# Decoder kernel on one core: the causal mask moves to VectorE, normalisations are pipelined, and the cross attention's softmax goes by row tiles

## The chip, the cores and the metric

The kernel runs on one core of a Trainium2 chip. The metric is device time in microseconds for one execution of the whole program, taken as the median of several runs. TensorE (PE) does the matmuls, VectorE (DVE) and ScalarE (ACT) the elementwise work, GpSimd (POOL) copies, powers and indirect DMAs, and SyncE (SP) issues most DMAs.

## What is computed

Two decoder layers over x of 8 sequences x 256 tokens x 256 features. Each layer is an attention, a second (cross) attention and a routed feed-forward part, each fed by a layer normalisation and added to x:

```
x = x + L0_attn(layernorm(x))            # causal self attention, 16 heads, 4 key heads, head size 128
x = x + L0_xattn(layernorm(x), ctx)      # top-2 of 64 context rows
x = x + L0_ffn(layernorm(x))             # 16 experts, 4 chosen
x = x + L1_attn(layernorm(x))            # gated delta rule, 64-step state
x = x + L1_xattn(layernorm(x), ctx)      # cross attention, keys = 64 context rows + 256 tokens
x = x + L1_ffn(layernorm(x))             # 128 experts, 48 kept, 8 chosen

def _layernorm(x, eps=1e-05):
    return (x - mean(x)) / sqrt(var(x) + eps)

# L0_attn
scores = einsum('bkgqd,bksd->bkgqs', qg, k) * scale
causal = triu(full((S, S), -inf), k=1)
attn = softmax(scores + causal)
out = einsum('bkgqs,bksd->bkgqd', attn, v)

# L1_xattn
q = rope(rms_norm(q, q_norm_w)); k = rope(rms_norm(k, k_norm_w))
probs = softmax(einsum('bhqd,bhkd->bhqk', q, k) * SCALE)
attn = einsum('bhqk,bhkd->bhqd', probs, v)
```

## The kernel before

Everything is in 32-bit floats. x lies in SBUF as 16 row tiles of 128 tokens. The program is a row of blocks, with all engines meeting between two blocks; within a block each engine has its own queue, in the order in which the code is written, and semaphores tie the queues together. There is no scheduler: the order of the code is the order of the queues.

`layernorm` (L155) is called six times, in 4 turns of 4 row tiles. A turn is one chain: VectorE's statistics (L181, L184) and the add of epsilon (L186), GpSimd's power for the reciprocal root (L200), VectorE's four normalisations (L191), eight transposes on TensorE into two PSUM banks (L213), and ScalarE's copy to `xnT` (L223). VectorE begins a turn's normalisations only when the transposes of the turn before have been made, and the transposes of a turn begin when its copy of the turn before is stored.

`attention` (L271) serves both the self attention (`cross` false) and the cross attention (`cross` true). A unit is one group of 4 query heads with one key head, for one sequence; there are 32 units, two at a time in buffers h = 0 and 1. The function `schedule` gives every engine the same row of stages. `stage(h, front, back)` does the front half of one unit (projections, rotation, and in the cross attention the root mean square of queries and keys, then transposes of queries and keys) and the back half of the unit before it, in the other buffer (scores, softmax, transposes of the probabilities, the product with the values, the output product). So a stage takes one unit forward, and there are some 32 of them in each attention.

In the back half the heads go by pairs, 0 and 1, then 2 and 3. On TensorE: scores of two heads, a projection of the front unit, the transposes of the probabilities (`turn_probs`, L460), the product with the values (`mix`, L470), then the same for heads 2 and 3, and `give` (L478). On VectorE: `row_max` for two heads (L588 in the cross attention, L594 in the self attention), which makes `mx` and the negated bound `nb`; ScalarE's `exps` (L684) writes `probs` and its row sums `den`; VectorE's `norm_probs` (L602 reciprocal, L605 multiply); `keep_probs` on VectorE (L614, L616) and ScalarE (L691, L694) copies the transposed probabilities out of PSUM. VectorE's `rotate` (L540 to L542) stands between the pairs for the queries, and for keys and values (part `TB`) between the normalisations of head 2 and head 3. ScalarE's `keep_v` (L666 to L671) waits for this last rotation and stands between its copies of the probabilities of heads 2 and 3.

A head's scores are two row tiles of 128 queries. In the cross attention each has 320 keys. In the self attention tile 0 sees 128 keys and tile 1 sees 256; both tiles lie in one PSUM bank, and the causal mask gets there first, by a bf16 matmul of an identity with a table of zeros and -1e30 (L448), onto which the score matmuls accumulate. In the cross attention GpSimd raises 15 columns of sums of squares to the power -1/2 (L388); VectorE's `rms_keys` (L576, L580) waits for it, and the transposes of queries and keys (L434, L437) wait for `rms_keys`.

## Time and profile before

| what | us |
|---|---|
| median of 3 runs (4133.5 to 4137.38) | 4135.25 |
| the profiled execution, its own time | 4131.25 |
| its span | 4129.5 |
| TensorE busy / VectorE busy / ScalarE busy / GpSimd busy | 3545.6 / 2634.8 / 1641.9 / 1414.0 |
| self attention, 26.47 to 664.00: TensorE / VectorE / ScalarE busy | 576.0 / 387.4 / 254.6 |
| 100 us of the cross attention, 3200 to 3300: TensorE / VectorE / ScalarE busy | 90.2 / 61.7 / 41.2 |
| first layer normalisation, 0 to 26.47: TensorE / VectorE busy | 7.8 / 13.1 |

The span is cut into stages: first normalisation to 26, self attention to 666, set attention to 759, routed experts from 780 to 1120, delta attention to 2882, cross attention from 2935 to 3861, sparse experts to the end. The second to sixth normalisations lie between these. A wait is read from a row's square bracket: how long the engine was idle ahead of it, and which engine's instruction ended that. TensorE's clock was granted in full (1.00) throughout both attentions' steady parts.

### The profile page before, as it was taken

The page shows a single profiled execution, that of the slowest core. Times are in us where ns is not written, and L with a number is a line of the kernel's source. Part 1 is how long each engine was busy: PE and PEld are TensorE (multiplying, and loading weights), DVE is VectorE, ACT ScalarE, POOL GpSimd, SP SyncE. Part 2 cuts the span into 40 slices and gives each one's busy share as a digit, 9 for nine tenths or more (in the row PEclk, how much of TensorE's full clock was granted, in tenths as well). Part 3 has the DMA queues.
Part 4 walks back from the last instruction along what each step waited for, and adds up shares of the span by engine and source line. Part 5 has one row for each costly group of instructions (what it writes and reads, how often), then busy time and mean ns, then how long its engine had stood idle before and what let it go on. Part 6 is the DMA issues. An engine that isn't in the chain of part 4 may idle for free. (4 is left out here: it accounts for less than half of the span.)

```text
span 4129.5 us, 57677 instructions
## 1 busy us (share of the span) xinstructions
PE 3545.6 (86%) x17488; PEld 2734.0 (66%) x17488; DVE 2634.8 (64%) x7558; ACT 1641.9 (40%) x4218; POOL 1414.0 (34%) x2085
## 2 busy tenths in 40 slices
PE   7999996589677999999999999997499999999564
PEld 5667665455365888888888888886355556556453
DVE  5666665532247888888888888873666666666531
ACT  3444432133234445555455554541244444444221
POOL 0000000068515555555555555552111111111055
PEclk9999998599869999999999999999699999999666
DMA  2000003345500111111111111110100000000346
GB/s 76 0 0 0 0 0 88 96 71 85 115 12 20 41 25 40 30 35 36 29 37 27 38 28 38 26 21 20 48 1 0 0 0 0 0 0 0 117 111 143
DMA packets 220951, 150.05 MB, mean 36 GB/s; under 512 B 116976, under 2 KB 208656, under 8 KB 220208
## 3 DMA queue, kind: packets, MB, share of 16 engines
q1 hardware_dynamic: 193664, 111.55, 10.4%
q0 software_dynamic: 22848, 31.69, 4.7%
q10 hardware_dynamic: 4224, 4.19, 0.3%
q8 instruction: 104, 1.70, 0.2%
q14 instruction: 111, 0.91, 0.1%
HBM read 105.71 MB, written 41.61 MB: 36 GB/s over the span
## 5 line engine op out<-in xcount | busy, mean ns | idle before, releaser
L1926 DVE SCALAR_TENSOR_TENSOR dl_y<-ps,dl_taps,dl_y 128x255 f32<-128x255 f32 (+2 forms) x1536 | 653.1, 475 | 129.5 <-ACT dl_y L1822 125.3
L1657 PE MATMUL ps<-xnT,dl_wkqv 128*128 128x256 f32 x2048 | 540.7, 390 | 32.4 <-DVE dl_lp L1969 22.3
L1657 PEld LDWEIGHTS ps<-xnT,dl_wkqv 128*128 128x128 f32 x2048 | 366.9, 193 | 83.9 <-issue 37.2
L388 POOL TENSOR_TENSOR at_rs<-at_ss,mhalf 128x15 f32<-128x15 f32 x32 | 125.5, 3922 | 744.8 <-DVE at_ss L571 744.8
L1580 POOL TENSOR_TENSOR dl_rn<-dl_n,mhalf 128x4 f32<-128x4 f32 x128 | 173.5, 1355 | 550.6 <-DVE dl_n L1942 550.6
L470 PE MATMUL ps<-at_shared,at_v 128*128 128x256 f32 (+2 forms) x1280 | 314.2, 378 | 4.6
L1822 ACT ACTIVATE dl_y<-ps,dl_taps 128x256 f32<-128x256 f32 x512 | 260.1, 560 | 101.0 <-PE ps L1657 101.0
L414 PE MATMUL ps<-at_wq,at_xb 128*128 (+1 forms) x512 | 244.4, 611 | 36.0 <-POOL at_xb L382 33.9
L1598 POOL TENSOR_TENSOR dl_inv_u<-dl_inv_u,dl_inv_tmp 64x30 f32<-64x30 f32 (+14 forms) x480 | 260.0, 542 | 37.6
L470 PEld LDWEIGHTS ps<-at_shared,at_v 128*128 128x128 f32 (+1 forms) x1280 | 209.7, 189 | 88.8 <-issue 64.0
L450 PE MATMUL ps<-at_kT,at_qT 128*128 128x320 f32 (+2 forms) x1024 | 257.7, 385 | 1.4 <-ACT at_kT L676 1.4
L460 PE MATMUL ps<-ident,at_probs 128*128 128x128 f32 (+1 forms) x1152 | 172.3, 281 | 100.2 <-DVE at_probs L605 100.2
L478 PE MATMUL ps<-at_wo,at_oT 128*128 (+1 forms) x1024 | 234.8, 382 | 18.7 <-ACT at_oT L699 18.7
L1682 PE MATMUL ps<-dl_wo,dl_z 128*128 128x256 f32 x1024 | 243.2, 380 | 0.0
L1595 POOL TENSOR_TENSOR dl_inv_tmp<-dl_inv_u,dl_inv_a 64x30 f32<-64x30 f32 (+14 forms) x480 | 234.2, 488 | 24.7
L460 PEld LDWEIGHTS ps<-ident,at_probs 128*128 128x128 f32 (+1 forms) x1152 | 122.9, 134 | 173.5 <-DVE at_probs L605 160.6
L1830 ACT ACTIVATE dl_z<-dl_y 128x512 f32<-128x512 f32 x256 | 161.6, 631 | 190.5 <-DVE dl_y L1926 190.5
L380 POOL COPY at_xb<-xnT 128x512 f32 (+1 forms) x64 | 39.2, 612 | 560.8 <-PE ps L422 556.0
L478 PEld LDWEIGHTS ps<-at_wo,at_oT 128*128 128x128 f32 x1024 | 189.4, 190 | 54.7 <-issue 27.5
L1668 PE MATMUL ps<-dl_z 128*128 128x512 f32 (+1 forms) x512 | 224.0, 520 | 0.0
L588 DVE TENSOR_REDUCE at_mx<-ps 128x2 f32<-128x640 f32 x128 | 105.6, 825 | 180.3 <-PE ps L450 176.7
L450 PEld LDWEIGHTS ps<-at_kT,at_qT 128*128 128x128 f32 x1024 | 169.3, 191 | 68.6 <-ACT at_kT L676 11.9
(348 smaller groups left out, 7755.5 us busy)
## 6 DMA issues: line engine op xcount, KB each, us to landing
dl_grow<-decay_rows SPq DMA_DIRECT2D x128, 128.0 KB, 3.0
sp_wgu<-in_w1gu SPq DMA_DIRECT2D x12, 768.0 KB
dl_wkqv<-in_w1kqv SPq DMA_DIRECT2D x16, 512.0 KB, 4.6
delta_diag<-dl_lp SPq DMA_DIRECT2D x512, 8.0 KB
dl_diag<-delta_diag_tt SPq DMA_DIRECT2D x512, 8.0 KB, 1.7
moe_wgu<-in_w0gu SPq DMA_DIRECT2D x16, 448.0 KB, 11.5
sp_wd<-in_w1d SPq DMA_DIRECT2D x12, 384.0 KB
dl_wo<-in_w1o SPq DMA_DIRECT2D x16, 256.0 KB, 3.7
```

The costliest lines, as they stand in the source:

```text
L414: last = nc.tensor.matmul(k.ps[h][:, t, :], xb[h][:, c, t * P:(t + 1) * P], wq[:, c, ds(group(u) * (G * HD), G * HD)], start=c == 0, stop= ...
L450: last = nc.tensor.matmul(scores(h, r, t), qT[h][:, r, t * P:(t + 1) * P], kT[h][:, 0:seen(t)], start=cross, stop=cross or t == TB - 1)
L460: last = nc.tensor.transpose(slot(h, (r % 2) * 4 + pieces[j])[0:w, t * P:(t + 1) * P], probs[h][:, (r % 2) * TB + t, j * P:j * P + w], k.i ...
L470: last = nc.tensor.matmul(slot(h, (r % 2) * 4 + 3)[:, c0:S], v[h][0:w, j, :], pT[h][0:w, r % 2, j, c0:S], start=j == 0, stop=j == KT - 1)
L478: last = nc.tensor.matmul(slot(h, t), oT[h][:, hh, t * P:(t + 1) * P], wo[:, ds(group(u) * G + hh, 1), :], start=hh == 0, stop=hh == G - 1)
L1595: nc.gpsimd.tensor_tensor(tmp, inv_u[:, 0:i, i:i + 1].to_broadcast([GP, i, w]), inv_a[:, i:i + 1, i + 1:Q32].to_broadcast([GP, i, w]), ALU ...
L1598: nc.gpsimd.tensor_tensor(inv_u[:, 0:i, i + 1:Q32], inv_u[:, 0:i, i + 1:Q32], tmp, ALU.subtract)\
L1657: last = nc.tensor.matmul(bank(h, m // 2, (m % 2) * S, (m % 2 + 1) * S), wkqv[h][:, c, m * P:(m + 1) * P], k.xnT[:, c, u.seq * S:(u.seq + ...
L1668: last = nc.tensor.matmul(bank(h, blk, 0, 2 * (S - blk * P)).rearrange("p (a s) -> p a s", a=2), z[h][:, 0, blk * P:(blk + 1) * P], z[h][: ...
L1682: last = nc.tensor.matmul(bank(h, 3, t * D, (t + 1) * D), z[h][:, 2 + m, t * P:(t + 1) * P], wo[h][:, m, :], start=m == 0, stop=m == 1)
L1822: last = nc.scalar.activation(y[h][:, m, :], bank(h, m // 2, (m % 2) * S, (m % 2 + 1) * S), ACT.Identity, bias=taps[h][:, m, KC:KC + 1], s ...
L1926: last = nc.vector.scalar_tensor_tensor(y[h][:, m, back:S], bank(h, m // 2, (m % 2) * S, (m % 2 + 1) * S - back), taps[h][:, m, KC - 1 - b ...
```

## The change

Four things change.

1. `layernorm` is pipelined: the statistics of turn i+1 are issued ahead of the normalisations of turn i, the small tiles are doubled, VectorE normalises two of the four row tiles and ScalarE the other two (an Identity activation with scale and bias, for which VectorE makes a shift, `ln_nmr`), and the transposes alternate between two pairs of PSUM banks.
2. In the self attention the mask matmul is gone. VectorE makes the maximum with an instruction that adds an f32 mask to the scores, writes the sums to `probs` in SBUF and reduces them to the maximum; ScalarE's exponential then reads `probs` in SBUF instead of PSUM, in place. The second row tile's scores have a bank of their own.
3. In the cross attention maximum, exponential, normalisation and transposes go by row tile with a semaphore step each, and GpSimd's power is split in two, of 1 and of 10 columns.
4. In both, the fourth head's normalisation stands ahead of the rotation of keys and values.

The core of the diff:

```diff
 def layernorm(k, rows=None, send=None):
-                dve.wait_ge(k.ln_turned, i + base + 1)
-                dve.wait_ge(k.ln_pow, i + base + 1)
-                for q in range(Q):
+            def normalise(i):
+                n, b = i + base, i % 2
+                if n >= 1:
+                    dve.wait_ge(k.ln_normed_a, n)
+                    dve.wait_ge(k.ln_turned_d, n)
+                dve.wait_ge(k.ln_pow, n + 1)
+                nc.vector.scalar_tensor_tensor(k.ln_nmr[b][:, HQ:Q], k.ln_mv[b][:, HQ:Q, 0], -1.0, k.ln_rstd[b][:, HQ:Q],
+                                               ALU.mult, ALU.mult).then_inc(k.ln_shift, 1)
+                for q in range(HQ):
...
+            stats(0)
+            for i in range(turns):
+                if i + 1 < turns:
+                    stats(i + 1)
+                normalise(i)
...
+            for i in range(turns):
+                n, b = i + base, i % 2
+                if n >= 1:
+                    act.wait_ge(k.ln_turned_a, n)
+                if first:
+                    act.wait_ge(k.x_loaded[i], 16)
+                act.wait_ge(k.ln_shift, n + 1)
+                for q in range(HQ, Q):
+                    last = nc.scalar.activation(xn(i, q), k.x[:, i * Q + q, :], ACT.Identity,
+                                                bias=k.ln_nmr[b][:, q:q + 1], scale=k.ln_rstd[b][:, q:q + 1])
+                last.then_inc(k.ln_normed_a, 1)
+                if i >= 1:
+                    keep(i - 1)
+            keep(turns - 1)
...
 # attention, GpSimd
-                    nc.gpsimd.tensor_tensor(rs[h][:, :, :], ss[h][:, :, :],
-                                            k.mhalf[:, 0:KT * (G + 1)].rearrange("p (t g) -> p t g", t=KT), ALU.pow)\
+                    nc.gpsimd.tensor_tensor(rs[h][0:CTX, TB, G:G + 1], ss[h][0:CTX, TB, G:G + 1], k.mhalf[0:CTX, 0:1], ALU.pow)
+                    nc.gpsimd.tensor_tensor(rs[h][:, 0:TB, :], ss[h][:, 0:TB, :],
+                                            k.mhalf[:, 0:TB * (G + 1)].rearrange("p (t g) -> p t g", t=TB), ALU.pow)\
                         .then_inc(s.rms_ready[h], 1)
...
 # attention, TensorE
-                    if not cross:
-                        nc.tensor.matmul(k.ps[h][:, (r % 2) * TB, 0:P + S], k.identb[:, :], k.causb[:, :], start=True, stop=False)
                     for t in range(TB):
                         last = nc.tensor.matmul(scores(h, r, t), qT[h][:, r, t * P:(t + 1) * P],
-                                                kT[h][:, 0:seen(t)], start=cross, stop=cross or t == TB - 1)
-                    last.then_inc(s.scored[h], 1)
+                                                kT[h][:, 0:seen(t)], start=True, stop=True)
+                        if cross:
+                            last.then_inc(s.scored[h], 1)
+                    if not cross:
+                        last.then_inc(s.scored[h], 1)
...
 # attention, VectorE
+                def tile_max(h, u, r, t):
+                    dve.wait_ge(s.scored[h], u * (G * TB) + (r * TB + t + 1))
+                    m = (r % 2) * TB + t
+                    link(h, u, f"max{r}{t}", nc.vector.tensor_reduce(mx[h][:, m:m + 1], scores(h, r, t), AX_X, ALU.max))
+                    nc.vector.scalar_tensor_tensor(nb[h][:, m:m + 1], mx[h][:, m:m + 1], -1.0,
+                                                   esc[h][:, t, r:r + 1], ALU.mult, ALU.mult).then_inc(s.max_ready[h], 1)
...
+                def head_max(h, u, r):
                     dve.wait_ge(s.scored[h], u * G + (r + 1))
                     b = (r % 2) * TB
+                    dve.sem_inc(s.masking[h], 1)
+                    for t in range(TB):
+                        last = nc.vector.tensor_tensor_reduce(probs[h][:, b + t, 0:seen(t)], scores(h, r, t),
+                                                              k.causal[:, S - seen(t):S], 1.0, NEG, ALU.add, ALU.max,
+                                                              mx[h][:, b + t:b + t + 1])
...
+                def softmax(h, u, r):
+                    if cross:
+                        tile_max(h, u, r, 0)
+                        tile_max(h, u, r, 1)
+                        tile_max(h, u, r + 1, 0)
+                        norm_tile(h, u, r, 0)
+                        tile_max(h, u, r + 1, 1)
+                        norm_tile(h, u, r, 1)
+                        norm_tile(h, u, r + 1, 0)
+                        norm_tile(h, u, r + 1, 1)
+                    else:
+                        head_max(h, u, r)
+                        head_max(h, u, r + 1)
+                        norm_head(h, u, r)
+                        norm_head(h, u, r + 1)
...
                     if back is not None:
-                        row_max(g, back, 2)
-                        row_max(g, back, 3)
-                        norm_probs(g, back, 2)
+                        softmax(g, back, 2)
                     if front is not None:
                         rotate(h, front, TB)
                     if back is not None:
-                        norm_probs(g, back, 3)
                         keep_probs(g, back, 2)
                         keep_probs(g, back, 3)
...
 # attention, ScalarE
-                    act.wait_ge(s.max_ready[h], u * G + (r + 1))
                     for t in range(TB):
+                        if cross:
+                            act.wait_ge(s.max_ready[h], u * (G * TB) + (r * TB + t + 1))
+                        elif t == 0:
+                            act.wait_ge(s.max_ready[h], u * G + (r + 1))
                         m = (r % 2) * TB + t
+                        source = scores(h, r, t) if cross else probs[h][:, m, 0:seen(t)]
```

VectorE's queue in the self attention, heads 2 and 3 of a stage, before (`at_mx` the maxima, `at_nb` the negated bounds, `at_t` the rotated halves of the front unit, `at_shared` the transposed probabilities):

```order
L594 TENSOR_REDUCE at_mx<-ps 128x1 x2
L596 TENSOR_SCALAR at_nb<-at_mx 128x2
L602 RECIPROCAL at_rden<-at_den 128x2
L605 TENSOR_SCALAR at_probs<-at_probs,at_rden 128x128
L605 TENSOR_SCALAR at_probs<-at_probs,at_rden 128x256
L540 TENSOR_TENSOR at_t<-ps,rope_cos 128x2x128
L541 TENSOR_TENSOR at_t<-ps,rope_sin 128x2x64
L542 TENSOR_TENSOR at_t<-ps,rope_sin 128x2x64
L602 RECIPROCAL at_rden<-at_den 128x2
L605 TENSOR_SCALAR at_probs<-at_probs,at_rden 128x128
L605 TENSOR_SCALAR at_probs<-at_probs,at_rden 128x256
L616 COPY at_shared<-ps 128x128 x2
```

The first two rows stand for head 3; head 2's are the same two ahead of them. The same place in the changed kernel, from head 3's maximum on:

```order
L650 ISA at_probs,at_mx<-ps,causal 128x128
L650 ISA at_mx 128x1
L650 ISA at_probs,at_mx<-ps,causal 128x256
L650 ISA at_mx 128x1
L654 TENSOR_SCALAR at_nb<-at_mx 128x2
L660 RECIPROCAL at_rden<-at_den 128x2
L662 TENSOR_SCALAR at_probs<-at_probs,at_rden 128x128
L662 TENSOR_SCALAR at_probs<-at_probs,at_rden 128x256
L660 RECIPROCAL at_rden<-at_den 128x2
L662 TENSOR_SCALAR at_probs<-at_probs,at_rden 128x128
L662 TENSOR_SCALAR at_probs<-at_probs,at_rden 128x256
L587 TENSOR_TENSOR at_t<-ps,rope_cos 128x2x128
```

Each reduction has become two instructions, the add-and-maximum and one that writes `at_mx` alone, and both normalisations stand ahead of the rotation.

VectorE's queue in the cross attention, heads 2 and 3 of a stage, before:

```order
L588 TENSOR_REDUCE at_mx<-ps 128x2
L590 SCALAR_TENSOR_TENSOR at_nb<-at_mx,at_esc 128x2
L588 TENSOR_REDUCE at_mx<-ps 128x2
L590 SCALAR_TENSOR_TENSOR at_nb<-at_mx,at_esc 128x2
L602 RECIPROCAL at_rden<-at_den 128x2
L605 TENSOR_SCALAR at_probs<-at_probs,at_rden 128x320 x2
L540 TENSOR_TENSOR at_t<-ps,rope_ck 128x2x128
```

And in the changed kernel, from head 3's first tile on, that is after two maxima and bounds of head 2's tiles:

```order
L634 TENSOR_REDUCE at_mx<-ps 128x1
L635 SCALAR_TENSOR_TENSOR at_nb<-at_mx,at_esc 128x1
L641 RECIPROCAL at_rden<-at_den 128x1
L642 TENSOR_SCALAR at_probs<-at_probs,at_rden 128x320
L634 TENSOR_REDUCE at_mx<-ps 128x1
L635 SCALAR_TENSOR_TENSOR at_nb<-at_mx,at_esc 128x1
L641 RECIPROCAL at_rden<-at_den 128x1
L642 TENSOR_SCALAR at_probs<-at_probs,at_rden 128x320
L641 RECIPROCAL at_rden<-at_den 128x1
L642 TENSOR_SCALAR at_probs<-at_probs,at_rden 128x320
L641 RECIPROCAL at_rden<-at_den 128x1
L642 TENSOR_SCALAR at_probs<-at_probs,at_rden 128x320
```

A head's reduction, bound and reciprocal are now one for each row tile, and all four normalisations stand ahead of `rotate`.

## Rows read from the trace of the kernel before

**Rows 1.** Timeline, second layer normalisation (start us, us, engine line op tiles, [idle <-releaser])

```profile
667.51 1.41 DVE L181 BATCH_NORM_STATS2 ln_stats<-x 128x6 f32<-128x256 f32 x4 [0.90 <-PEq L99]
...
669.36 0.17 DVE L186 TENSOR_SCALAR ln_ve<-ln_mv 128x4 f32<-128x4 f32 x1
...
669.61 1.01 POOL L200 TENSOR_TENSOR ln_rstd<-ln_ve,mhalf 128x4 f32<-128x4 f32 x1 [67.48 <-DVE ln_ve L186]
...
670.74 1.38 DVE L191 TENSOR_SCALAR ln_xn<-x,ln_mv,ln_rstd 128x256 f32<-128x256 f32 x4 [1.21 <-POOL ln_rstd L200]
...
672.17 1.97 PE L213 MATMUL ps<-ident,ln_xn 128*128 128x128 f32 x8 [6.29 <-DVE ln_xn L191]
...
687.70 1.01 ACT L223 COPY xnT<-ps 128x1024 f32<-128x1024 f32 x1 [3.49 <-PE ps L213]
```

**Rows 2.** Busy time by stretch; DMA share is the last number but one

```profile
22.00:24.00 2.00, 0.85 (x4) 0.85 (x5) 1.09 (x4) 0.00 (x0) 0.00 (x0) 1.00 0.87 277
```

**Rows 3.** Timeline, first projection of the self attention

```profile
27.22 5.59 PE L414 MATMUL ps<-at_wq,at_xb 128*128 128x512 f32 x8 [2.10 <-POOL at_xb L380]
```

**Rows 4.** Timeline, one stage of the self attention

```profile
301.83 0.82 PE L460 MATMUL ps<-ident,at_probs 128*128 128x128 f32 x6
...
307.77 0.21 ACT L684 ACTIVATION_READ_ACCUMULATOR at_probs<-ps,at_nb 128x1 f32 x1
307.87 0.42 DVE L540 TENSOR_TENSOR at_t<-ps,rope_cos 128x256 f32<-128x256 f32 x1
...
309.40 0.55 PE L460 MATMUL ps<-ident,at_probs 128*128 128x128 f32 x3 [0.84 <-DVE at_probs L605]
...
309.99 0.29 DVE L616 COPY at_shared<-ps 128x128 f32<-128x128 f32 x1 [0.44 <-PE ps L460]
...
311.73 1.09 PE L434 MATMUL ps<-ident,at_t 128*128 128x128 f32 x8 [0.40 <-DVE at_t L558]
...
316.33 0.33 PE L448 MATMUL ps<-causb,identb 128*128 128x384 bf16 x1
...
316.50 0.82 PE L450 MATMUL ps<-at_kT,at_qT 128*128 128x128 f32 x4
...
320.18 0.55 DVE L605 TENSOR_SCALAR at_probs<-at_probs,at_rden 128x128 f32<-128x128 f32 x2
...
321.40 0.82 PE L460 MATMUL ps<-ident,at_probs 128*128 128x128 f32 x6
```

**Rows 5.** VectorE's groups by line and shape: xcount | busy us, mean ns | idle

```profile
L594 DVE TENSOR_REDUCE at_mx<-ps 128x1 f32<-128x256 f32 x128 | 53.1, 415 | 0.0
...
L541 DVE TENSOR_TENSOR at_t<-ps,rope_sin 128x256 f32<-128x256 f32 x64 | 26.6, 415 | 0.0
...
L1276 DVE DVE_READ_ACCUMULATOR moe_picked<-moe_xs,moe_pick 128x1 f32 x79 | 6.5, 83 | 0.0
```

**Rows 6.** ScalarE's groups by line and shape, same columns

```profile
L1842 ACT ACTIVATE dl_dec<-dl_gm,dl_ng 128x256 f32<-128x256 f32 x128 | 64.9, 507 | 0.0
...
L684 ACT ACTIVATE at_probs<-ps,at_nb 128x256 f32<-128x256 f32 x128 | 60.1, 470 | 0.0
```

**Rows 7.** Timeline, one stage of the cross attention

```profile
3310.07 0.82 DVE L588 TENSOR_REDUCE at_mx<-ps 128x2 f32<-128x640 f32 x1 [1.51 <-PE ps L450]
...
3311.15 0.82 DVE L588 TENSOR_REDUCE at_mx<-ps 128x2 f32<-128x640 f32 x1
...
3312.47 0.17 DVE L602 RECIPROCAL at_rden<-at_den 128x2 f32<-128x2 f32 x1 [0.30 <-ACT at_probs L684]
...
3312.67 0.68 DVE L605 TENSOR_SCALAR at_probs<-at_probs,at_rden 128x320 f32<-128x320 f32 x2
...
3315.38 0.87 PE L460 MATMUL ps<-ident,at_probs 128*128 128x128 f32 x6 [1.10 <-DVE at_probs L605]
...
3318.63 3.92 POOL L388 TENSOR_TENSOR at_rs<-at_ss,mhalf 128x15 f32<-128x15 f32 x1 [23.52 <-DVE at_ss L571]
...
3323.86 1.09 PE L434 MATMUL ps<-ident,at_t 128*128 128x128 f32 x8 [0.16 <-DVE at_t L580]
```

159 lines of the change are left out of this document (86 added, 73 removed).

## The prediction, made before the result was known

> **What bounds the kernel now.** I read the busy time by stretch first (the table above: TensorE is the busiest engine of both attentions, at some 90%), then the timeline of one stage of each kind, looking only at which wait ends last. Work taken off TensorE can shorten the self attention, but only as far as VectorE's chain allows, and the reader is to see how that chain divides a stage. A stage (four heads of one sequence, 32 stages) lasts 19.57 us: transposes of the probabilities start at 301.83 and again at 321.40 [rows 4]. In it TensorE waits for VectorE 0.84 us at 309.40 and 0.40 us at 311.73, while the next stage's transposes at 321.40 show no wait. So the stage has two parts: from 301.83 to 311.73 (9.90 us) VectorE's queue ends last; from 311.73 to 321.40 (9.67 us) TensorE's does. The cross attention (32 stages of 28.2 us) is alike, with TensorE waits of 1.10 us for the probabilities and 0.16 us for the keys [rows 7]. The six layer normalisations are serial: in each of 4 turns every engine waits for the one before it, 21.2 us in all (667.51 to 688.71) [rows 1].
>
> **Layer normalisation (six calls).** Today a turn passes statistics, power, four normalisations, eight transposes and a copy one after another, with VectorE idle 1.2 us for GpSimd [rows 1]. The change does the next turn's statistics in that gap, gives two of the four normalisations to ScalarE, and alternates PSUM banks. The chain now: statistics to the add of epsilon start 1.85 us apart (667.51 to 669.36), with that add's own 0.08 about 1.93. Two of these come before the first shift instruction: 3.86. Then each turn costs VectorE 1.93, a shift of some 0.1 and two normalisations at 0.33 apart (1.38 for four): 2.69. The third turn's shift is at 3.86 + 2 x 2.69 = 9.24, its two normalisations end at 10.1. Four transposes take 1.11 (eight take 1.97, so 0.21 each and 0.47 for the last). The last turn has to wait for the row buffers: VectorE until 11.2, ScalarE until the other four transposes end, 12.1. ScalarE's two normalisations, 0.51 each and overlapping [rows 6], end at 13.1, four transposes at 14.3, the copy (1.01) at 15.3. Gain 21.2 - 15.3 = 5.9 us a call. Five calls have nothing else that ends last in them: 29.5. In the first call the loads take over: the DMA engines are still busy 0.87 of 22 to 24 us, with the attention's weights last, so the first projection, now at 27.22, can't start before about 24.1 [rows 2, 3]: gain 3.1, not 5.9. Sum 32.6 us (28 to 35; the gains repeat six times the same reckoning, so I take 1 us a call as its error, less where two errors cancel).
>
> **Self attention, TensorE's part.** 128 mask matmuls go, four a stage. Each holds the queue 0.17 us (316.33 to the next matmul at 316.50) though its row says 0.33 [rows 4]. The two ahead of scores 0 and 1 lie in the part that TensorE bounds: -0.33 us. The two ahead of scores 2 and 3 lie in the part that VectorE bounds, and there scores are waited for by nobody: 0. What is late next is VectorE: its last probabilities of this part are done at 320.73 (320.18 + 0.55), and the transposes that need them start behind three others of 0.11, at 321.73: 1.0 us of cover, less weight loads of about 0.3 and the 0.33 of the masks, leaves 0.3 to 0.4.
>
> **Self attention, the new pass.** A maximum per head was two reductions; now it is two add-and-maximum instructions with a written result, each followed by an instruction that reads the accumulator. The trace has no such instruction. From below: an add with a PSUM operand takes 415 ns for 256 elements, a maximum 415 ns as well [rows 5], so the pass itself might cost 0 more, and no reason says less. The accumulator read takes 83 ns where one occurs [rows 5], partly under its predecessor: 0.07 to 0.17 a head. From above: if the unknown instruction takes two cycles an element, the head's 384 elements cost 0.4 us more (at 1.05 ns an element, from 415 ns for 256 to 820 for 640 [rows 5, 7]). I take 0.12 us a head, since both row kinds of the same shape agree to the nanosecond. The Trainium skill ("Vector Engine (DVE) Microarchitecture Reference", Measured stream behaviour on trn2) says that multi-step programs pay the same fixed cost as built-in ones; no row here shows it. By it the self attention would gain 13 to 14 us. ScalarE's exponential now reads SBUF: 507 against 470 ns at 256 elements [rows 6], +0.035 an instruction, +0.07 a head.
>
> **Self attention, VectorE's part.** The fourth head's normalisation moves ahead of the rotation of keys and values. Its exponential ends at 307.98 (307.77 + 0.21), 0.11 after VectorE is free (307.87), so the move costs a wait of 0.15; it removes the wait of VectorE for the fourth transposes (0.44 at 309.99) [rows 4]: -0.29. The new pass and the exponentials put 0.12 + 0.07 back through the chain maximum, exponential, reciprocal: -0.29 + 0.19 = -0.10. The rotation now ends 0.8 later, ScalarE's copy of the values waits for it, and the last copy of probabilities stands behind that copy; mixing heads 2 and 3 still ends 0.2 us before the keys' transposes may start, so it costs nothing yet. In TensorE's part 2 x 0.19 = 0.38 is added to VectorE's chain against that cover of 0.3: 0.05 to 0.1 late. Stage: -0.33 + 0.07 - 0.10 = -0.36, times 32 = **-11.5 us**. Each further 0.1 us a head first costs 0.2 a stage (two heads in TensorE's part, while VectorE's part waits for the exponentials), so at 0.3 a head the gain is gone; past that all four heads count, 0.4 a stage. Bounds: -20 (pass, reads and exponentials free, -0.62 a stage) and +26 (two cycles an element, 0.5 a head with the reads: 0.2 x 4 x 32).
>
> **Cross attention.** A maximum of two row tiles takes 0.82 and the next starts 1.08 after it [rows 7]. One tile has 320 elements less: 1.08 - 320 x 1.05 ns = 0.74, negated bound and all. Normalising a head holds VectorE 0.80 today: 0.20 from the reciprocal to the first multiply (3312.47 to 3312.67) and about 0.30 for each multiply (0.68 for two, the last 0.08 under the next instruction) [rows 7]; a tile 0.50. A pair of heads costs 4 x 0.74 + 4 x 0.50 = 4.96, before 2 x 1.08 + 2 x 0.80 = 3.76: +1.20 us of VectorE. Against it, the first maximum starts one row tile of scores earlier (320 columns in four passes, -0.53), and VectorE's waits for exponentials (0.3 a head) fill: -0.3 to -0.6. The transposes follow tile by tile, so after the last tile only four of six are left: 0.24 less. First pair: +1.20 - 0.53 - 0.6 - 0.24 = -0.2. Second pair: the fourth head's normalisation again passes the rotation (here six instructions of 64 to 256 columns, about 1.2 us by 415 ns for 256); both probability sets are transposed 0.9 us earlier (the 1.10 us wait at 3315.38 falls to 0.3), but VectorE's copy of them stands behind the rotation, so mixing starts at the same time as before. The rotation ends 1.2 us later, ScalarE's three squares (about 1.4 us: 1.01 for 1,024 columns as in the copy of [rows 1], 0.4 for the rest) start later by as much, and the last probability copy queues behind them: mixing head 3 waits 0.35 to 0.45. The squares make the sums 0.6 late; the power shrinks from 15 columns (3.92) to 10 and 1. From 1.01 for 4 and 3.92 for 15 [rows 1, 7] it is 0.26 a column, so 2.6 + 0.3 = 2.9: 1.0 earlier, 0.4 net. The keys' wait (0.16, with 0.2 of drain) goes: -0.35. Sum -0.2 + 0.4 - 0.35 = -0.15, times 32 = **-5 us**, bounds -16 and +14 (each unknown 0.1 to 0.3 a stage).
>
> The Trainium skill ("VectorE: DVE Perf Modes", Rules for kernel authors) says to minimise the number of VectorE operations; the tile split does the opposite. By that rule rival (b) below is what happens, and the sum would be -12 instead of -49.
>
> **Sum.** -32.6 - 11.5 - 5 = -49 us. The profiled execution took 4131.25 us (span 4129.5); that gives 4082 for it, and 4086 against the median of 4135.25. I name 4084.
>
> **Rivals.** (a) The add-and-maximum is dear (two cycles an element or a fixed 0.2 us more each): self +26 instead of -11.5, total -12: 4123. For it: no row of its kind. Against: every two-operand row streams at one element a cycle. (b) VectorE's added instructions in the cross attention land on the path: of +1.20 us a pair about half stays in both pairs, +1.0 a stage after the gains: +32 instead of -5, total -12: 4123. For it: 1.20 us is more than the wait ahead of the reciprocal that it fills (0.30). Against: VectorE idles 1.51 us ahead of even the second pair's first maximum [rows 7], a third of which the earlier tile uses. (c) Slower than before: the same mechanism as (a) with a larger price. Past 0.3 us a head each further tenth is on the path four times a stage, 12.8 us in all; from 0.3 + 0.29 = 0.59 us a head (0.3 an instruction with its read) the loss eats the 37.6 us from elsewhere, and at 0.8 us a head the kernel takes 4135 - 38 + 64 = 4161 us. (d) The normalisations gain half, because ScalarE's share or the barriers end last: total -33: 4102.
>
> **How the numbers follow.** Forecast 0.62, (a) 0.12, (b) 0.08, (c) 0.04, (d) 0.14. The range 4064 to 4116 takes in the forecast with its bounds (-20 and -16 don't fall together with 35) and (d); (a), (b) and (c) lie mostly above. A measurement here can tell about 0.2% (8 us). Faster: all but (c) and a small part of (a) and (b): 0.92; within: 0.04; slower: 0.04, which is (c).
>
> **What would show it.** Layer normalisation calls of about 15.3 us, and the first projection at about 24 us with the DMA engines just ending. The add-and-maximum rows at 0.28 and 0.42 us; over 0.5 at 256 elements is (a). A self stage of 19.2 us with no wait at the first transposes; a cross stage of 28.1 us, with a new wait of ScalarE ahead of the squares and of TensorE ahead of mixing head 3, and no wait at the keys. A cross stage over 28.5 is (b). The forecast is wrong if a stage of either attention is longer than before.

## The result, and the profile of the changed kernel

The changed kernel takes **4096.1 us** (median of 3 runs, 4095.19 to 4096.52) against 4135.25 before: the ratio is 0.9905, with a 95% interval of 0.9891 to 0.9919. That is 39 us faster. The forecast was 4084, 51 us faster, with a range of 4064 to 4116. The sign and the range held; 12 us of the gain are missing.

The profiled execution has a span of 4093.9 us, 35.6 less than before. Between landmarks that both traces have (the first statistics of each layer normalisation, and the end of its last copy into the transposed activations) it divides so:

| stretch | before, us | changed, us | difference |
|---|---|---|---|
| first normalisation | 21.25 | 15.59 | -5.66 |
| its end to the end of the self attention | 641.35 | 648.88 | **+7.53** |
| the other five normalisations, together | 106.08 | 78.93 | -27.15 |
| set attention | 70.55 | 67.89 | -2.66 |
| routed experts | 341.11 | 343.54 | +2.43 |
| delta attention | 1739.22 | 1740.52 | +1.30 |
| rotary tables and cross attention | 958.83 | 945.09 | -13.74 |
| sparse experts to the end | 246.20 | 248.61 | +2.41 |

The self attention, which was to gain 11.5 us, is longer by 7.5. The cross attention gained nearly three times the 5 us of the forecast.

**The normalisations.** The timeline of the third call (start us, us, engine, line, tiles, and in brackets the idle time before the instruction and what ended it), to be read beside [rows 1]:

```profile
752.90 1.41 DVE L184 BATCH_NORM_STATS2 ln_stats<-x 128x6 f32<-128x256 f32 x4 [0.32 <-PEq L857]
...
756.92 0.16 DVE L199 SCALAR_TENSOR_TENSOR ln_nmr<-ln_mv,ln_rstd 128x2 f32<-128x2 f32 x1
...
757.18 1.09 ACT L259 ACTIVATE moe_rows<-x,ln_nmr,ln_rstd 128x256 f32<-128x256 f32 x2 [8.64 <-DVE ln_nmr L199]
...
764.56 0.16 DVE L199 SCALAR_TENSOR_TENSOR ln_nmr<-ln_mv,ln_rstd 128x2 f32<-128x2 f32 x1 [1.33 <-PE ps L234]
...
765.35 1.09 ACT L259 ACTIVATE moe_rows<-x,ln_nmr,ln_rstd 128x256 f32<-128x256 f32 x2 [0.69 <-PE ps L240]
...
767.65 1.01 ACT L249 COPY xnT<-ps 128x1024 f32<-128x1024 f32 x1 [0.31 <-PE ps L240]
```

The chain is the one of the forecast. The first shift instruction comes 4.02 us after the start (forecast 3.86), the last one 11.66 us after it (11.2), and the copy ends at 15.76 (15.3). ScalarE's two normalisations take 1.09 us, where 1.0 was assumed. The first projection starts at 24.41, ended by a DMA, instead of 27.22 [rows 3]:

```profile
24.41 2.08 PE L451 MATMUL ps<-at_wq,at_xb 128*128 128x512 f32 x2 [5.02 <-DMA at_wo<-in_w0o]
```

**The self attention.** One stage in the timeline, to be read beside [rows 4]:

```profile
301.93 0.82 PE L500 MATMUL ps<-ident,at_probs 128*128 128x128 f32 x6
...
305.52 0.28 DVE L650 CUSTOM_DVE_ANT_0 at_probs<-ps,causal 128x128 f32<-128x128 f32 x1
305.73 0.08 DVE L650 DVE_READ_ACCUMULATOR2_ANT at_mx<- 128x1 f32 x1
305.73 0.42 DVE L650 CUSTOM_DVE_ANT_0 at_probs<-ps,causal 128x256 f32<-128x256 f32 x1
...
306.19 0.17 DVE L654 TENSOR_SCALAR at_nb<-at_mx 128x2 f32<-128x2 f32 x1
...
306.44 0.29 DVE L650 CUSTOM_DVE_ANT_0 at_probs<-ps,causal 128x128 f32<-128x128 f32 x1
...
307.61 0.94 DVE L662 TENSOR_SCALAR at_probs<-at_probs,at_rden 128x128 f32<-128x128 f32 x2
...
307.79 0.62 POOL L420 COPY at_xb<-xnT 128x512 f32 x1 [18.73 <-PE ps L459]
...
308.61 1.20 PE L500 MATMUL ps<-ident,at_probs 128*128 128x128 f32 x6 [1.03 <-DVE at_probs L662]
...
308.66 0.55 DVE L662 TENSOR_SCALAR at_probs<-at_probs,at_rden 128x128 f32<-128x128 f32 x2
...
310.28 1.55 PE L514 MATMUL ps<-at_shared,at_v 128*128 128x256 f32 x8 [0.47 <-DVE at_shared L689]
...
311.79 1.09 PE L471 MATMUL ps<-ident,at_t 128*128 128x128 f32 x8
```

The same place before the change:

```profile
305.41 0.61 DVE L594 TENSOR_REDUCE at_mx<-ps 128x1 f32<-128x128 f32 x2
306.06 0.17 DVE L596 TENSOR_SCALAR at_nb<-at_mx 128x2 f32<-128x2 f32 x1
306.15 0.62 DVE L594 TENSOR_REDUCE at_mx<-ps 128x1 f32<-128x128 f32 x2
```

The add-and-maximum instructions take 0.28 and 0.42 us, hardly more than plain maxima (0.415 for 256 columns [rows 5]). In the queue a head still costs VectorE more: from its pass to the next head's it is 0.92 us (305.52 to 306.44) against 0.74 before (305.41 to 306.15), and 0.94 against 0.82 for the pair of heads in TensorE's part. That is 0.12 to 0.18 us a head, where 0.12 was forecast; rival (a) had 0.4 and is out. The first transposes (301.93) do not wait. This stage is as forecast. But not all are. Here is the length of each stage from the sixth on, from one addition of the attention's output on VectorE to the next, as worked out from the timeline (us):

```
before   19.57 19.58 19.56 19.59 19.57 19.57 19.57 19.59 19.57 19.58 19.56 19.59 19.57 19.58 19.57 19.58
changed  19.15 19.36 19.15 19.35 19.15 20.85 19.14 19.36 19.15 20.85 19.15 19.41 19.15 20.86 19.14 19.37
```

Stages of 19.15 and 19.36 us alternate, 19.25 in the mean, 0.32 less than before. Nine of the 31 stages between the additions last 20.64 to 20.91 instead, about 1.5 us more, and the last stage has 1.4 us of the same. One stage with a fall by microsecond (us, then the busy time of TensorE, its weight loads, VectorE, ScalarE and GpSimd, then the granted TensorE clock as a share of 2.4 GHz, DMA share, GB/s):

```profile
503.00:504.00 1.00, 0.17 (x1) 0.00 (x0) 0.96 (x3) 0.90 (x4) 0.62 (x1) 1.00 0.00 0
504.00:505.00 1.00, 0.69 (x4) 0.46 (x5) 0.96 (x5) 0.22 (x1) 0.00 (x0) 1.00 0.00 0
505.00:506.00 1.00, 0.53 (x4) 0.32 (x4) 1.00 (x6) 0.60 (x3) 0.00 (x0) 0.96 0.00 0
506.00:507.00 1.00, 1.00 (x3) 0.82 (x4) 1.00 (x1) 0.21 (x1) 0.00 (x0) 0.50 0.00 0
507.00:508.00 1.00, 1.00 (x5) 0.91 (x4) 0.33 (x1) 0.37 (x1) 0.00 (x0) 0.50 0.00 0
...
509.00:510.00 1.00, 1.00 (x9) 1.00 (x8) 0.00 (x0) 0.14 (x1) 0.00 (x0) 0.83 0.00 0
510.00:511.00 1.00, 1.00 (x7) 0.90 (x6) 0.00 (x0) 0.78 (x1) 0.00 (x0) 1.00 0.00 0
```

TensorE waited for the third head's probabilities (0.17 busy in the first row), then for the mixing, and at about 505.9 its clock fell from 2.4 to 1.2 GHz for 3.4 us. The mixing, 1.55 us in the stage above, was hit by it:

```profile
505.87 2.86 PE L514 MATMUL ps<-at_shared,at_v 128*128 128x256 f32 x8 [0.47 <-DVE at_shared L689]
```

Before the change the clock stood at 1.00 in all of the steady stages of the self attention. A window of ten stages tells it in one number, the last but two of the row (before, then changed):

```profile
100.00:300.00 200.00, 183.14 (x920) 139.15 (x919) 123.72 (x399) 80.82 (x277) 6.17 (x10) 1.00 0.00 0
```

```profile
100.00:300.00 200.00, 182.62 (x874) 137.22 (x873) 128.04 (x481) 84.38 (x275) 6.19 (x10) 0.97 0.00 0
```

So the stretch's +7.53 is: -0.32 x 31 = -9.9 for the stages, 9 x 1.5 + 1.4 = +14.9 for ten falls of the clock, and +2.9 for the first projection's wait for its weights (3.97 us after the first call's last copy, 1.06 before). The sum is +7.9.

**The cross attention.** Its stages last 27.76 and 28.05 us in turn, 27.90 in the mean; before 28.09 and 28.39, 28.24. Nowhere in them did the clock fall. Thirty stages make 10.1 of the 13.74 us, and 0.5 lies ahead of them. The other 3.1 are in the last stage, which has no front half (28.17 us before, 25.09 now). Before the change the clock fell once in it, from 3840.4 to 3843.8; the same stage by whole heads and without a fall took 26.67 us in the run with whole heads below, so about 1.5 of the 3.1 us are that fall and not the change. The second half of a steady stage, to be read beside [rows 7]:

```profile
3341.01 2.42 PE L485 MATMUL ps<-at_kT,at_qT 128*128 128x320 f32 x8
...
3341.86 0.49 DVE L634 TENSOR_REDUCE at_mx<-ps 128x1 f32<-128x320 f32 x1 [1.26 <-PE ps L485]
...
3347.57 1.02 ACT L733 ACTIVATE at_shared<-ps 128x1024 f32<-128x1024 f32 x1 [0.84 <-DVE at_t L589]
...
3348.01 1.73 PE L514 MATMUL ps<-at_shared,at_v 128*128 128x256 f32 x6 [0.95 <-DVE at_shared L687]
...
3349.05 1.49 DVE L615 TENSOR_REDUCE at_ss<-at_shared 128x10 f32<-128x1280 f32 x1 [0.85 <-ACT at_shared L735]
...
3351.06 1.73 POOL L428 TENSOR_TENSOR at_rs<-at_ss,mhalf 64x1 f32<-64x1 f32 x1 [23.43 <-DVE at_ss L618]
...
3352.76 1.96 POOL L429 TENSOR_TENSOR at_rs<-at_ss,mhalf 128x10 f32<-128x10 f32 x1
3354.68 0.60 POOL L420 COPY at_xb<-xnT 128x512 f32 x1
...
3354.75 0.56 DVE L623 TENSOR_SCALAR at_esc<-at_rs 128x8 f32<-128x8 f32 x1 [2.17 <-POOL at_rs L429]
...
3356.04 0.86 PEld L471 LDWEIGHTS ps<-ident,at_t 128*128 128x128 f32 x8 [0.43 <-DVE at_t L627]
3356.04 1.10 PE L471 MATMUL ps<-ident,at_t 128*128 128x128 f32 x8
```

The predicted signs are all there: the wait of ScalarE ahead of the squares (0.84), one of TensorE ahead of the fourth head's mixing, though only 0.24 us long, and no wait for the keys. The matmuls at 3356.04 follow the ones before them within 0.03 us, where they waited 0.16 [rows 7]. The 0.43 in the row above is the idle time of the weight loads; it was 0.51 to 0.56 us before. Two of the expectations below call this 0.43 a wait of TensorE; it is not one that the change brought. A wait that nobody forecast is the 0.95 ahead of the third head's mixing: the transposes of the probabilities come earlier, and VectorE's copy of them stands behind the rotation. The power of a single column on 64 partitions takes 1.73 us, not the 0.3 of the forecast, so what the division gives is small.

### The profile page after: what moved, and what is told of

The parts are those of the page before. It is cut to its first block and busy times, and to the rows that moved or that the text cites. A ratio compares the mean times of both kernels' runs of the same rounds, so it can differ in the third digit from the quotient of the medians.

```text
span 4093.9 us, 59202 instructions
## 1 busy us (share of the span) xinstructions
PE 3563.6 (87%) x17360; PEld 2733.3 (67%) x17360; DVE 2677.0 (65%) x8174; ACT 1688.1 (41%) x4266; POOL 1407.6 (34%) x2115
## 5 line engine op out<-in xcount | busy, mean ns | idle before, releaser
L514 PE MATMUL ps<-at_shared,at_v 128*128 128x256 f32 (+2 forms) x1280 | 332.3, 393 | 56.4 <-DVE at_shared L687 29.4
L428 POOL TENSOR_TENSOR at_rs<-at_ss,mhalf 64x1 f32<-64x1 f32 x32 | 55.4, 1731 | 742.1 <-DVE at_ss L618 742.1
L485 PE MATMUL ps<-at_kT,at_qT 128*128 128x320 f32 (+2 forms) x1024 | 249.9, 387 | 2.8 <-ACT at_kT L743 2.8
L634 DVE TENSOR_REDUCE at_mx<-ps 128x1 f32<-128x320 f32 x256 | 125.3, 489 | 146.0 <-PE ps L485 145.9
L1753 PEld LDWEIGHTS ps<-dl_wo,dl_z 128*128 128x128 f32 x1024 | 196.8, 192 | 27.8 <-issue 0.2
L1941 ACT COPY dl_wv<-ps 128x256 f32<-128x256 f32 x256 | 95.4, 373 | 283.4 <-PE ps L1814 189.9
L485 PEld LDWEIGHTS ps<-at_kT,at_qT 128*128 128x128 f32 x1024 | 167.3, 191 | 67.1 <-ACT at_kT L743 13.6
```

The lines of the kernel that those rows point to most:

```text
L485: last = nc.tensor.matmul(scores(h, r, t), qT[h][:, r, t * P:(t + 1) * P], kT[h][:, 0:seen(t)], start=True, stop=True)
L514: last = nc.tensor.matmul(slot(h, (r % 2) * 4 + 3)[:, c0:S], v[h][0:w, j, :], pT[h][0:w, r % 2, j, c0:S], start=j == 0, stop=j == KT - 1)
L1753: last = nc.tensor.matmul(bank(h, 3, t * D, (t + 1) * D), z[h][:, 2 + m, t * P:(t + 1) * P], wo[h][:, m, :], start=m == 0, stop=m == 1)
```

## The experiments

Theory, after the comparison of the traces: the normalisations gave about 30 us; the self attention's stages gave 10 and falls of TensorE's clock took 15 back; the cross attention gave 11 to 14. The chief rival: the falls are chance, or come from the shorter normalisations, and the missing gain lies elsewhere. Each ratio is to the kernel before on the same chip. Two things limit them. The delta attention, which nobody touched, lasted between 1731 and 1749 us in the profiled runs, with 78 to 118 us at the lower clock, and the runs of one kernel spread by up to 18 us. The lengths of undisturbed stages agree within 0.02 us between kernels with the same attention, and most verdicts rest on them.

### The normalisations alone

The kernel before, with the layer normalisation function of the changed one and its buffers and semaphores.

> The kernel before with the six layer normalisations of the changed one and nothing else. In the trace of the changed kernel five calls last 15.7 to 15.9 us instead of 21.2 and the first projection starts 2.8 us earlier: 5 x 5.4 + 2.8 = 29.9. If what follows a call does not care when it ends, this kernel is 30 us faster than before (4105). If part of it is given back behind the calls (the phase of the routed experts is 2.4 us longer in the changed kernel, the last phase 2.4 us, the delta attention 1.3 us, the set attention 2.7 us shorter), it is 26 to 27 us (4108 to 4109).

Measured: 4117.98 us, ratio 0.9945 (0.9929 to 0.9962), so 16 to 29 us faster. The five later calls last 15.7 to 16.2 us and the self attention's stages 19.57 as before, without one fall of the clock. In this run the delta attention was the longest of all (1749.09 us, 118 us at the lower clock), 10 us above the trace of before. The calls and the loads account for 29 us in its trace, whose span is only 18 us shorter. The trace shows where the rest went: 9.9 us in the delta attention and 5.8 in the cross attention (964.59 against 958.83), of which 4.7 are its last stage, with the clock at the lower level for 13.7 us of it. Neither part's code was touched. For the median, which gained 22 us, it was not shown.

### Normalisations and self attention, cross attention of before

The cross attention's softmax by heads, its order and its one power of 15 columns are restored.

> The changed kernel with the cross attention as it was before (whole heads, fourth normalisation behind the rotation, one power of 15 columns): so the normalisations and the self attention alone. Theory: the self attention's stage is 0.23 us shorter, 7.4 us in all, but TensorE's clock falls to its lower level nine times more than before, for 3.4 us each, which costs about 1.3 us each, 12 us: this kernel is 4 to 5 us slower than the one with the normalisations alone, and the cross attention's part of the change is the rest, some -14 us. Rival: the falls come from something else than the change of the self attention (the shorter normalisation, the day's state of the chip): then this kernel is 7 us faster than the one with the normalisations alone, or the falls stand in that one too.

Measured: 4113.26 us, ratio 0.9933 (0.9917 to 0.995). The stretch of the self attention is 651.00 us against 644.09 in the kernel with the normalisations alone, 6.9 us more, and eight of its stages last over 20.6 us. The rival is out: the kernel with the normalisations alone has no fall, and the four traces with this self attention (this one, the changed kernel, and the two below with the power in one piece and with whole heads) have seven to nine such stages each. The cross attention is 959.77 us long, as before (958.83), and 945.09 in the changed kernel: its part of the change is worth 14 us in the traces, the luck of the last stage included. The two whole times are 5 us apart in the other direction, but their intervals overlap; in this run's profile the delta attention was 9.6 us shorter and the untouched cross attention 4.8. The theory's split holds in the traces; the ratios alone can't tell.

### A filler ahead of the scores

```
+ if not cross and r > 1:
+     nc.tensor.matmul(k.ps[h][:, (r % 2) * TB, 0:S], k.ident[:, :],
+                      k.causal[:, 0:S], start=True, stop=True)
  for t in range(TB):
      last = nc.tensor.matmul(scores(h, r, t), ...)
```

> The changed kernel with one more matmul ahead of the scores of the third and of the fourth head in the self attention: identity times mask, 256 columns, into the region that the scores overwrite at once, so that it computes nothing. It stands where two mask matmuls stood before. Theory: the clock falls because TensorE has too little to do around its two waits (1.03 and 0.47 us) in the second half of a stage; with the filler some or all nine falls of the self attention go, worth 1.3 us each, and the filler costs nothing or little since VectorE ends last there: -6 to -12 us against the changed kernel. Rival: the falls have another cause, and the filler only costs: 0 to +13 us (2 x 0.2 us in 32 stages).

Measured: 4099.34 us, ratio 0.9909 (0.989 to 0.9928), no gain. The theory is right on the clock and wrong on the price: no steady stage has a fall any more, but each is 19.54 or 19.96 us long, 0.50 more than undisturbed ones. That is more than the rival's 0.4. The timeline says why (filler L485, add-and-maximum L653):

```profile
303.46 0.67 PE L485 MATMUL ps<-causal,ident 128*128 128x256 f32 x2
...
304.97 0.29 DVE L653 CUSTOM_DVE_ANT_0 at_probs<-ps,causal 128x128 f32<-128x128 f32 x1 [0.21 <-PE ps L488]
...
306.06 0.29 DVE L653 CUSTOM_DVE_ANT_0 at_probs<-ps,causal 128x128 f32<-128x128 f32 x1 [0.24 <-PE ps L488]
```

VectorE now waits 0.21 and 0.24 us for the scores of the third and fourth head. There was next to no cover there: the filler removed the falls and cost as much.

### A filler in the wait itself

```
+ def fill(h, n):
+     for _ in range(n):
+         nc.tensor.matmul(k.ps[h][:, 3, 0:S], k.ident[:, :], k.causal[:, 0:S],
+                          start=True, stop=True)
  ...
  if back is not None:
+     if front is not None and not cross:
+         fill(h, 3)
      turn_probs(g, back, 2)
```

> The changed kernel with three matmuls (identity times mask, 256 columns, some 0.22 us each) that TensorE does in the self attention between the projection of keys and values and the transposes of the third head's probabilities, where it waits 1.03 us. They write a PSUM bank that nobody uses at that time and compute nothing. Theory: ten stages of the changed kernel's self attention last 20.65 to 20.91 us instead of 19.15 and 19.36, since TensorE's clock falls in them, because of what it leaves undone in the second half; three matmuls in a wait that is there anyway cost nothing, and no stage or nearly none has a fall: 10 x 1.5 = 15 us faster than the changed kernel, ratio to before 0.987. Rival: the filler delays VectorE's work as the one ahead of the scores did (0.5 us a stage): then stages of 19.4 to 19.9 us and no gain, ratio 0.990. Or the falls stay, since the engine must be busy elsewhere: ratio 0.9905.

Measured: 4083.63 us, ratio **0.9873** (0.9848 to 0.9897), 13 us less than the changed kernel. The intervals of the two ratios just overlap, so the claim rests on the trace. The steady stages are 19.14 and 19.36 us, to 0.01 those of the undisturbed ones of the changed kernel, and none has a fall. The stretch of the self attention is 634.12 us, 14.8 less than 648.88. The filler and the clock of the stretch (the first row is the three matmuls, two records each in the trace; the transposes behind them start at 300.82, so they hold TensorE for 1.29 us, 0.43 each, where the expectation had 0.22):

```profile
299.53 1.46 PE L494 MATMUL ps<-causal,ident 128*128 128x256 f32 x6
```

```profile
100.00:300.00 200.00, 193.27 (x957) 148.67 (x956) 131.93 (x496) 86.91 (x285) 6.27 (x11) 1.00 0.00 0
```

This is the missing gain. TensorE was busy 10 us longer in these 200 us, nothing of it useful, and the kernel is faster. The falls came with what TensorE left undone in the second half of a stage.

### The old order of the self attention, without and with the filler

```
  norm_head(h, u, r)
- norm_head(h, u, r + 1)
+ if r == 0:
+     norm_head(h, u, r + 1)
  ...
  rotate(h, front, TB)
+ if back is not None and not cross:
+     norm_head(g, back, 3)
```

> The changed kernel with the fourth head's normalisation of the self attention back behind the rotation of the keys; the mask stays in VectorE's pass. Theory: TensorE's waits in the second half are split again into three smaller ones (before: 0.30, 0.84 and 0.40 us), so the clock holds; the stage is about as long (the second half gained only 0.04 us from the order), so this kernel is 8 to 12 us faster than the changed one. Rival (the one of the forecast): the order is worth 0.1 to 0.3 us a stage and the clock has nothing to do with it: 3 to 10 us slower than the changed one.

Measured: 4118.31 us, ratio 0.9951 (0.9934 to 0.9968), 19 us slower than the changed kernel. Both theories are wrong here. The first of TensorE's waits did not shrink to 0.30 us: it is 0.99 to 1.03, as in the changed kernel, and two more follow, 0.83 and 0.40. GpSimd's copy still runs beside the third head's multiply (the copy at 336.86, the two multiplies 0.90 us from 336.73). And the order is worth far more than 0.1 to 0.3 us a stage. Twenty stages last 20.6 us or more and the clock is lower still:

```profile
100.00:300.00 200.00, 178.87 (x838) 136.44 (x837) 126.64 (x470) 81.71 (x267) 6.16 (x10) 0.94 0.00 0
```

> The changed kernel with the old order of the self attention and the three matmuls of filler in TensorE's wait, so the mask's move alone without falls of the clock. In the run with the old order and no filler 23 stages had a fall and the others lasted 19.33 to 19.93 us, too few and too scattered to tell its own length. Theory: 19.45 to 19.65 us, no gain over the 19.57 of before, since the second half's chain grew by what the first half lost; no falls. Ratio 0.989 to 0.990. Rival: the mask's move alone is worth its 0.33 less 0.07 of the forecast: stages of 19.3, ratio 0.988.

Measured: 4097.89 us, ratio 0.9902 (0.9885 to 0.9919). No steady stage has a fall, and they are 19.68 and 19.89 us long, 19.78 in the mean: **0.21 longer than before**. That is past the top of the range I gave. The undisturbed stages of the run without the filler have the same lengths (19.68 and 19.89 to 19.94), so the filler is not what lengthens them. Moving the mask to VectorE without the new order makes the stage longer.

### The new order with the mask on TensorE

The kernel with the new normalisations alone, and in it:

```
  norm_probs(g, back, 2)
+ if not cross:
+     norm_probs(g, back, 3)
```

> The kernel before with the new layer normalisations and the new order of the self attention (fourth head's normalisation ahead of the rotation of the keys), but the mask still added by TensorE and the maximum still a plain reduction. So the order alone. Theory: the order is worth more than the 0.29 less 0.19 of the forecast, 0.3 us a stage, and the mask's move only what is left of the 0.32: stages of 19.25 to 19.35 us instead of 19.57, and, as the four mask matmuls keep TensorE busy, no falls of the clock: 7 to 10 us faster than the kernel with the new normalisations alone, ratio 0.9925. Rival (the forecast's sum): the order gives 0.1 us at most and the mask's move 0.2: stages of 19.45 to 19.55, ratio 0.994.

Measured: 4097.09 us, ratio 0.9897 (0.988 to 0.9913), although its cross attention is that of before. Its steady stages last 19.25 and 19.31 us, 19.28 in the mean, none with a fall. In the second half TensorE waits in three pieces, and after each there is work:

```profile
301.76 0.55 PE L503 MATMUL ps<-ident,at_probs 128*128 128x128 f32 x3 [0.30 <-DVE at_probs L648]
302.69 0.55 PE L503 MATMUL ps<-ident,at_probs 128*128 128x128 f32 x3 [0.38 <-DVE at_probs L648]
303.70 1.55 PE L513 MATMUL ps<-at_shared,at_v 128*128 128x256 f32 x8 [0.47 <-DVE at_shared L659]
```

With these the undisturbed stage of the self attention is known for all four combinations:

| | old order | new order |
|---|---|---|
| mask on TensorE | 19.57 | 19.28 (-0.29) |
| mask on VectorE | 19.78 (+0.21) | 19.25 (-0.32) |

The order does it. The mask's move adds 0.03 us a stage to the order's 0.29, 1 us in all, and brings the ten falls of the clock, 15 us. Without the move, the self attention's stretch is 635.65 us instead of 648.88.

The two parts of a stage show why the move gives so little. TensorE's part goes from the keys' transposes to the next transposes of the probabilities, VectorE's part from there to the keys' transposes (means of undisturbed stages, us):

| | TensorE's part | VectorE's part |
|---|---|---|
| before | 9.67 | 9.90 |
| new order, mask on TensorE | 9.67 | 9.61 |
| new order, mask on VectorE (changed) | 9.42 | 9.83 |
| old order, mask on VectorE, filler | 9.40 | 10.36 |

The move takes 0.25 us from TensorE's part and puts 0.22 into VectorE's, or 0.46 with the old order.

### The copy of the tokens held back

```
  wait_before(pool, s.projected[h], u * 3)
+ wait_before(pool, s.qk_kept[h], u)
  xc = nc.gpsimd.tensor_copy(xb[h][:, :, 0:S], ...)
```

> The changed kernel with GpSimd's copies of a sequence's tokens held back until ScalarE has kept the queries and keys of the sequence before in the same buffers (one more wait on GpSimd). The copy isn't needed until two stages later. Theory: in the self attention the copy now runs beside VectorE's multiply of 256 columns of the third head and makes it 0.39 us longer (0.94 instead of 0.55 for the two multiplies), on the path; in the cross attention it runs beside the scaling of 128x8 exponent factors (0.55 instead of about 0.17 us), ahead of which TensorE waits 0.43 us. Without the two: self stages of 18.9 to 19.0 us and cross stages of 27.5 to 27.6, 32 x (0.35 + 0.35) = 22 us faster, and fewer falls of the clock; ratio 0.985. Rival: the lengths of these two instructions have nothing to do with the copy: nothing changes, ratio 0.9905.

Measured: 4100.8 us, ratio 0.9914 (0.9898 to 0.9931), no gain. The cause was right for the self attention: the multiply of 256 columns falls from 429 to 347 ns in the mean of 128, which is 0.33 us in each stage. The stage gains only 0.10 of it (19.07 and 19.25 us), all in VectorE's part (9.73 instead of 9.83). And 16 stages had a fall instead of nine, which took more than it gave; the stretch is 654.98 us. TensorE's waits are shorter here, 0.64, 0.39 and 0.47 us, and the clock falls more often: the length of the waits alone doesn't tell when it falls. In the cross attention nothing changed, because the edit missed there: the copy still stood right behind the power in GpSimd's queue.

> Both edits together: the copy held back, two matmuls of filler in the wait ahead of the third head's transposes and one in the wait ahead of its mixing. If both theories hold, 15 + 22 = 37 us less than the changed kernel, ratio 0.9815; if the filler alone helps 0.987, if the copy alone helps 0.985.

Measured: 4088.91 us, ratio 0.9884 (0.9867 to 0.99). Stages of 19.06 and 19.25 without a fall, and a stretch of 634.81 us: 0.1 a stage less than with the filler alone, but 17.79 instead of 16.72 us for the last stage, where the clock fell. The delta attention (1749.28 us) hides the rest. As a whole it is no better than the filler alone, and both theories together had asked for 37 us.

### The power in one piece

> The changed kernel with GpSimd's power over all 15 columns at once again, as before. In the changed kernel the two powers take 1.73 (64x1) and 1.96 us (128x10) and start 1.70 us apart, so 3.65 us against 3.92 for the one. Theory: the split is worth 0.27 us a stage and no more, since VectorE and TensorE wait for it: 32 x 0.27 = 9 us slower than the changed kernel, ratio 0.9925. Rival (the forecast's price): the split is worth 1 us a stage before what the later squares take, so 0.9 to 1 us a stage slower, 30 us, ratio 0.998.

Measured: 4097.68 us, ratio 0.9915 (0.9895 to 0.9935). The cross attention's stages are 28.01 and 28.28 us long, 0.24 more than in the changed kernel, and its stretch 954.08 instead of 945.09. The theory was 0.27; the forecast's price of 1 us is refuted. TensorE's wait for the keys is back, 0.27 us in the mean. The whole time hardly shows it, as the delta attention was at its shortest in the profile (1730.83 us).

### Whole heads in the cross attention

The changed kernel with the pair of maxima, the normalisations and the transposes by head; the order and the divided power stay.

> The changed kernel with the cross attention's softmax by whole heads again, as before; the fourth head's normalisation stays ahead of the rotation and the power stays divided. Undisturbed stages of the cross attention so far: 28.24 us before, 27.90 changed, 28.14 changed with one power, so the division is worth 0.24 us and tiles and order together 0.10. Theory: the tiles are worth 0.2 us as forecast and the order costs 0.1: a stage of 28.1 us, 6 us slower than the changed kernel. Rival 1: the tiles are worth nothing (VectorE's added instructions take what the earlier start gives) and the order all of the 0.10: a stage of 27.9. Rival 2: the tiles cost and the order gives more: under 27.8.

Measured: 4117.27 us, ratio 0.9946 (0.993 to 0.9963), 17 us slower than the changed kernel. Stages of 28.46 and 28.75, 28.60 in the mean. Neither the theory nor a rival had this. Without the tiles, the new order and the divided power make the stage 0.36 us longer than before. The tiles give **-0.70**. If the divided power is worth the same -0.24 here as with tiles, the order by itself costs **+0.60**; no run has the order alone. The second half of its stage:

```profile
3349.35 2.42 PE L485 MATMUL ps<-at_kT,at_qT 128*128 128x320 f32 x8
...
3350.73 0.82 DVE L623 TENSOR_REDUCE at_mx<-ps 128x2 f32<-128x640 f32 x1 [1.52 <-PE ps L485]
...
3357.90 1.49 DVE L603 TENSOR_REDUCE at_ss<-at_shared 128x10 f32<-128x1280 f32 x1 [0.85 <-ACT at_shared L704]
```

From the start of the scores to that of the sums of squares it takes 8.55 us, in the changed kernel 8.04 (3341.01 to 3349.05), before 7.94 (3308.69 to 3316.63). So the order makes the sums 0.61 us later, which bears out its +0.60. From VectorE's first maximum to the sums it is 7.17 and 7.19 us: the same. So in this half the tiles give just the earlier start of the maximum, 0.5 us, and their added instructions cost nothing, since VectorE waited for exponentials anyway. The other 0.2 us are the first half's: from the keys' transposes to the scores of the third head it takes 13.07 us before, 13.06 here and 12.87 with tiles. The Trainium skill ("VectorE: DVE Perf Modes", Rules for kernel authors) says of chained VectorE operations to keep their number small; here the measurement says the contrary: twelve more VectorE instructions a stage (four maxima, four bounds, four reciprocals) make it 0.70 us shorter. Whether tiles with the old order would be better still was not run.

### Filler, and the copy later in both attentions

```
  def stage(h, front, back):
      if front is not None:
-         take_tokens(h, front)
          if cross:
              invert_rms(h, front)
+         pool.wait_ge(s.qk_kept[h], front + 1)
+         take_tokens(h, front + 1)
```

with the first two copies ahead of the loop, none for a sequence past the last, and the three matmuls of filler in the self attention.

> The changed kernel with the three matmuls of filler in TensorE's wait, and GpSimd's copy of the tokens done behind the keeping of queries and keys in both attentions, for the sequence after in the same buffers. In the run with the held copy the cross attention's copy still stood right behind the power, beside VectorE's scaling of 128x8 factors (0.55 us) and TensorE's wait (0.43 us) for it. Theory: without a copy beside it the scaling takes 0.17 us, the cross stage 27.90 - 0.35 = 27.55; self stages 19.06 and 19.25 as with the held copy: 14 us faster than the kernel with the filler alone, ratio 0.984. Rival: the scaling takes 0.55 us by itself: cross stages as they are, 3 us faster than the kernel with the filler alone, ratio 0.9865.

Measured: **4078.75 us**, ratio **0.9858** (0.9842 to 0.9874), the fastest of all: 19 us less than the changed kernel by the ratios. From the filler alone the intervals don't part it; the traces do. Cross stages of 27.55 and 27.79, 27.67 in the mean, 0.23 less; the stretch is 937.44 instead of 945.09. Self stages of 19.06 and 19.24. The theory had 27.55 for the cross stage: of the 0.39 us that the scaling gets shorter, 0.23 reach the stage. The scaling takes what the theory said, though it starts as late as before behind the power:

```profile
3226.68 0.17 DVE L642 TENSOR_SCALAR at_esc<-at_rs 128x8 f32<-128x8 f32 x1 [2.17 <-POOL at_rs L429]
...
3230.77 0.61 POOL L420 COPY at_xb<-xnT 128x512 f32 x1 [4.13 <-ACT at_kT L762]
```

The Trainium skill ("SBUF — State Buffer", Who interferes with whom) says that a GpSimd operation and a VectorE multiply or copy that reads and writes SBUF in its two-port mode can exclude each other for a whole instruction. The traces agree: 0.56 us beside the copy and 0.17 without, 0.94 beside it and 0.55 without for the pair in the self attention; and before the change the self attention's copy (from 307.94) ran beside a rotation that reads PSUM and cost it nothing (0.42 us at 307.87 [rows 4]). Which mode the instructions took, no run shows. The cross attention's scaling met the copy before the change too (0.55 us at 3322.58), so that loss is an old one.

## Why the forecast was right in sign and 12 us too low

**Layer normalisation: right in mechanism, a little too large.** The five calls gained 27.15 us, 5.43 each, against 5.9: the start took 0.16 more, each turn 2.75 (756.92 to 759.67) instead of 2.69, and the last turn's shift comes 0.46 late, as late as the copy's end. The first projection gained 2.81 against 3.1, with a DMA ending its wait as said. That is 30.0 instead of 32.6. Rival (d) did not happen.

**Self attention, undisturbed stage: right, term by term.** -0.32 measured, -0.36 forecast. TensorE's part was to gain 0.26 (-0.33 for the masks, +0.07 for VectorE late there) and gained 0.25. In VectorE's part the order was to give 0.29 and gives 0.29 (9.90 to 9.61), and the pass and the exponentials were to put 0.19 back and put back 0.22 (9.61 to 9.83). Each add-and-maximum pass costs 0.12 to 0.18 us a head against 0.12, each exponential 0.02 to 0.03 against 0.035 (493 ns against 470 at 256 columns). The mask's move was thus forecast at a net 0.07 and is worth 0.03; my expectation for the run with the mask on TensorE told the forecast's split wrongly. One piece of the 0.22 was not in the sum. GpSimd's copy, which stood beside a PSUM read before, now meets a multiply in SBUF; holding it back took 0.10 off the stage. The mask's move brings the two together and not the order: with the mask on VectorE the third head's pair takes 0.94 us in the old order too (307.21 in the run with the filler), with the mask on TensorE and the new order 0.55 (301.16) and the fourth head's, which the copy then meets, 0.67. In the old order nothing covers it, which is the likely reason for the 0.46 there.

**Self attention, the clock: the step that was missing.** The sum took TensorE's duration from rows at a clock of 1.00 and kept it there. Nothing in it asked what TensorE does when work is taken off it and its waits stay. It cost 14.9 us, more than the 9.9 that the stages gained. By the prediction's own last sign, no stage longer than before, its account of the self attention was wrong: nine stages of 31 are more than 1 us longer than 19.57. The four masks in a stage held TensorE 0.17 us each. With them, with the filler ahead of the scores or with the one in the wait, no steady stage had a fall; without any of these all six traces had them. None of my rivals had this mechanism, and (c), the one that ended slower, looked for the loss in VectorE's pass.

**Cross attention: twice the gain, from a sum of wrong terms.** Forecast -0.15 a stage, measured -0.34. The power was to fall from 3.92 to 2.9 and fell to 3.7 (3351.06 to 3354.72), and the division is worth 0.24; the wait for the keys went, as said. I had the price of one column from a line through 4 and 15 columns; the rows for 1, 4, 10 and 15 columns read 1.73, 1.01, 1.96 and 3.92, and no line goes through them. The order was to cost 0.4, through the mixing of the fourth head and the sums; it costs about 0.60, and what it delays by 0.6 are indeed the squares and their sums. The tiles were to give 0.2, in the first pair only. They give 0.2 there, and 0.5 more in the second pair, where the first maximum comes earlier too. Rival (b), that the added 1.20 us of VectorE land on the path, is out: none of it shows.

**Behind the calls.** Set attention, routed experts, delta attention and sparse experts together are 3.5 us longer than before, which was not in the sum. In the kernel with the normalisations alone the routed experts' stretch is 341.54 us and in the one with the mask on TensorE 341.27, in all with the mask on VectorE 342.3 to 343.5. What ties these 2 us to a mask that is used elsewhere stays open. The delta attention's 1.3 lie within its spread.

**The sum, and the luck in it.** In the traces the normalisations gave 30.0 us against 32.6, the self attention lost 4.7 against a gain of 11.5, the cross attention gave 13.7 against 5, and the rest lost 3.5 against nothing: 35.5 instead of 49. So the whole is 12 us off because one error of 16 us and one of 9 us go opposite ways, and the 9 us hold a fall of the clock before the change that has nothing to do with it. That the time fell into the range is in part luck. So is it that the kernel with the filler, at 0.9873 of 4135.25 or 4083 us, stands where the forecast did.

## What to carry to other kernels

Taking work off the engine that is busiest can slow it, if its clock then falls: before you remove cheap TensorE work, look at which waits stand around it, and read the granted clock stage by stage, not over the whole. A wait that is there anyway could be filled here at no cost with work that computes nothing (three matmuls in a wait of 1.03 us), while the same kind of work ahead of scores that VectorE waits for cost 0.50 us a stage. And price a combined edit by its parts: here the order and the tiles carried the gain, the mask's move carried 1 us and a loss of 15, and in the cross attention the order and the divided power without the tiles were a loss of 0.36 us a stage.

## What the hardware showed that was not expected

- TensorE's clock fell to 1.2 GHz for 3.4 us at a time in like stages, again and again but not in each. With waits of 1.03 and 0.47 us in a stage it fell in 9 of 31; with 1.0, 0.83 and 0.40 in 20; with 0.64, 0.39 and 0.47 in 16. With 0.30, 0.84 and 0.40 and four mask matmuls (before) it fell in none, though the waits add up to as much as in the first case; nor with 0.30, 0.38 and 0.47 and the masks. So idle time alone does not tell it here. A stage with a fall was 1.0 to 1.5 us longer.
- GpSimd's power took 1.73 us for 64x1, 1.01 for 128x4, 1.96 for 128x10 and 3.92 for 128x15. The first and the last stood behind 23 us of idleness, but the 1.01 stood behind 67 us of it [rows 1], so idleness by itself is not what makes them long. What does stays open.
- A copy on GpSimd made a VectorE instruction on 8 columns 0.39 us longer (0.56 against 0.17), more than twice its own length; the two multiplies of a head were 0.39 us longer beside it too (0.94 against 0.55).
- An add-and-maximum of VectorE with a PSUM operand and a written result took 0.42 us for 256 columns, as a plain maximum does (0.415). From one head to the next it was still 0.12 to 0.18 us more, for the next pass starts 0.25 us behind the bound (306.19 to 306.44), where the plain maximum started 0.09 behind it (306.06 to 306.15).
